# Middle stage of a fused two-layer transformer kernel: scale folded into the sign matrix, product evictions moved to ACT, second residual moved to POOL

## The chip, the cores and the metric

The kernel runs on one core of one Trainium2 chip. The metric is the device time of one execution in microseconds (us). The engines are PE (TensorE, with PEld its weight loads), DVE (VectorE), ACT (ScalarE), POOL (GpSimd) and SP, which here only issues DMAs and waits.

## What is computed

Two transformer layers on x of 4 batches, 512 tokens, 512 features, all fp32. Layer 0 has grouped causal attention with 32 heads of 128, and a feed-forward layer with a matrix of signs. Layer 1 has thresholded attention with 32 heads of 16 and a routed low-rank layer. The change is about the sign layer and the residual behind it:

```python
def _L0_ffn_ref(input, weight, scale_param):
    row_scale = jnp.clip(jnp.mean(jnp.abs(weight), axis=1), 1e-08, None)
    binary_weight = jnp.sign(weight / row_scale[:, None])
    out = jnp.einsum('bsi,oi->bso', input, binary_weight)
    out = out * row_scale[None, None, :] * scale_param[None, None, :]
    return jnp.nan_to_num(out, nan=0.0, posinf=1000000.0, neginf=-1000000.0)
...
h = _layernorm(x, axis=-1) * (1 + ca) + sa
x = x + ga * _L0_attn_ref(h, ...)
h = _layernorm(x, axis=-1) * (1 + cb) + sb
x = x + gb * _L0_ffn_ref(h, L0_ffn_weight, L0_ffn_scale_param)
...
h = _layernorm(x, axis=-1) * (1 + ca) + sa
q = (h @ Wq.T + bq)
```

## The kernel before

The batches are worked on in two halves of two. Each half goes through four stages with a barrier of all engines between them: `stage_first` (norm), `stage_groups` (attention of layer 0, by far the longest), `stage_middle` and `stage_heads_and_finish`. Only `stage_middle` is touched; it runs twice, from 846.5 us and from 1902.0 us. `x` and `y` are two SBUF buffers of eight tiles (128 tokens by 512 features each); they swap their names between the halves, so what is `y` in the first half is `x` in the rows of the second. Tiles 0 to 3 are batch 0 of the half, tiles 4 to 7 batch 1. Every engine runs its own list, written by hand, in order, and semaphores tie the lists together. There is no planner.

What `stage_middle` does in one half, tile by tile:

- The first residual, x = x + gate * attention output, is finished on DVE for tiles 4 to 7 (`summed(0, j)`: add L1319, `bn_stats` L1321); POOL does three of the gate products (L1284, semaphore `gated`).
- `normalise(i, b)` on DVE turns statistics of four tiles into mean and 1/sqrt(var) with a chain of small dependent instructions (L1341 to L1352) and raises `ready`.
- ACT's `features(i)` writes the normalised tiles (L1474), PE's `turn(i)` transposes them into PSUM (L1421), and ACT scales them on the way out (L1484; for i = 2 also L1486, the high part `hh`). Here i = 0, 1 are the inputs of the sign layer for batches 0 and 1, and i = 2, 3 those of the projections of layer 1. For i = 3 DVE writes the normalised tiles (L1382, `last_xn`).
- ACT makes the sign matrix `sgn` (L110, four slices). `signed(j)` on PE multiplies tile j with it into one of four PSUM banks `pF[j % 4]` (L1430, semaphore `full`). The order on PE is turn(0), signed(0), signed(1), turn(1), signed(2) to signed(7), turn(2), project(0) to project(6), turn(3), project(7) to project(23).
- `examine(j)` on DVE takes the product out of PSUM and multiplies it by the row scale `rs` (L1356, `z_done`, which also frees the bank), then finds NaN and infinities and replaces them (L1359 to L1365, `put`).
- POOL's `apply_gate(j)` multiplies by the second gate (L1280, `z_gated`), and DVE's `second_residual(j)` adds (L1319) and takes statistics (L1321). Behind the last tile of a batch comes `normalise(1, b)`.
- The weights of the three projections are split in a high part on ACT (`qkv.his`, L143, twelve casts) and a low part on POOL (`qkv.lo_of`, L146). POOL also makes the low part of the features (`low`, L1275, `h_lo`). `project(n)` on PE (L1450) is twelve matmuls; its first items wait slice by slice for `h_lo` and for `qkv.lo`.

The order of POOL's list and of DVE's around the sign layer, which the change touches:

```python
for j in range(TT):
    apply_gate(j)
for n in range(KT):
    qkv.lo_of(pool, n)
apply_gate(TT)
low(2, (0, 1))
apply_gate(TT + 1)
low(2, (2, 3))
apply_gate(TT + 2)
...
for j in range(TT, NT):
    first_residual(j)
normalise(0, 1)
```

Of the kernel before, what the change touches and what calls it, by code (L numbers as in the profile page):

```python
# [18 lines left out]
ALU = mybir.AluOpType  # L19
# [5 lines left out]
KT = D // P  # L25
# [93 lines left out]
class QkvWeights:  # L119
# [18 lines left out]
    def his(self, act):  # L138
        act.wait_ge(self.b_came, 48)
        for i in QKV_ORDER:  # L140
            act.wait_ge(self.came[i], 16)
            for k in range(KT):
                self.nc.scalar.copy(self.wh[:, i, k], self.raw[:, i, k]).then_inc(self.hi, 1)  # L143
# [1043 lines left out]
def stage_middle(nc, held, a, hf, signs, qkv, gates, later, kd0, half):  # L1187
# [3 lines left out]
    with Stage(nc, f"mid{half}") as st:  # L1191
# [15 lines left out]
        full, z_done, marked, replaced, put, z_gated = (st.sem(n) for n in (  # L1207
            "full", "z_done", "marked", "replaced", "put", "z_gated"))
# [30 lines left out]
        with nc.Block() as block:  # L1239

            @block.sync
            def _(sp):
                signs.load(sp)
                qkv.load(sp)
                for loaded in later:
                    loaded.load(sp)
                sp.wait_ge(own_gated, 1)
                sp.wait_ge(gated, TT - 1)
                load_gates(sp, held, a, 1, half, gate_in)
                sp.wait_ge(put, NT)  # L1250
                sp.dma_start(bo, a["b1o"].rearrange("(o d) -> o d", o=1).to_broadcast([P, D])).then_inc(bo_in, 16)
                for n, (w, b, m) in enumerate(items):
                    src = rest[n % NB]
                    if w == 2:
                        sp.wait_ge(left, n + 1)
                        for d in range(4):
                            sp.dma_start(a["vp"][b, :, :, 4 * m + d].rearrange("r g x -> g r x"),
                                         src[32 * d:32 * d + 32].rearrange("p (r x) -> p r x", r=4)).then_inc(stored[n % NB], 16)
                    else:
                        sp.wait_ge(flipped, kq[n] + 1)  # L1260
                        dst = a["kp" if w == 1 else "qp"][b, :, 4 * m:4 * m + 4].rearrange("j d l x -> (d l) j x")
                        sp.dma_start(dst, src.rearrange("p (j x) -> p j x", j=4)).then_inc(stored[n % NB], 16)
                for loaded in later:
                    loaded.landed(sp)
                for i in range(NB):
                    sp.wait_ge(stored[i], total[i])

            @block.gpsimd
            def _(pool):
# [7 lines left out]
                def apply_gate(j):  # L1277
                    pool.wait_ge(put, j + 1)
                    pool.wait_ge(gate_in, 16 * HB)
                    nc.gpsimd.tensor_tensor(y[:, j, :], y[:, j, :], gate[:, j // TT, :], ALU.mult).then_inc(z_gated, 1)  # L1280

# [28 lines left out]
            def _(dve):  # L1310
# [7 lines left out]
                def summed(i, j):  # L1318
                    nc.vector.tensor_tensor(x[:, j, :], x[:, j, :], y[:, j, :], ALU.add).then_inc(x_new, 1)  # L1319
                    dve.wait_ge(x_new, i * NT + j + 1 - TT)  # L1320
# [10 lines left out]
                def second_residual(j):  # L1331
                    dve.wait_ge(z_gated, j + 1)
                    summed(1, j)
# [20 lines left out]
                def examine(j):  # L1354
                    dve.wait_ge(full, j + 1)
                    nc.vector.tensor_tensor(y[:, j], pF[j % 4][:], rs[:], ALU.mult).then_inc(z_done, 1)  # L1356
# [12 lines left out]
                normalise(0, 1)  # L1369
                for b in range(HB):  # L1370
# [35 lines left out]
            def _(pe):  # L1406
# [17 lines left out]
                def signed(j):  # L1424
                    pe.wait_ge(signs.signed, KT)
# [41 lines left out]
            def _(act):  # L1467
                def features(i):
# [4 lines left out]
                    for j in range(b * TT, (b + 1) * TT if i < LAST else b * TT):  # L1473
                        nc.scalar.activation(y[:, j, :], x[:, j, :], ACT.Identity, bias=shifts[:, j:j + 1],  # L1474
                                             scale=scales[:, j:j + 1]).then_inc(xn_done, 1)
                    act.wait_ge(turned, i + 1)
# [31 lines left out]
                features(1)  # L1508
                qkv.his(act)
                features(2)  # L1510
                act.wait_ge(full, NT)
# [555 lines left out]
```

## Time and profile before

| what | value |
| --- | --- |
| median of 3 runs | 2157.39 us (2156.38 to 2159.48) |
| the profiled execution, its own time | 2156.57 us |
| its span, first to last instruction | 2154.6 us |
| busy share of the span: PE, DVE, ACT, POOL | 92%, 69%, 50%, 48% |
| middle stage, first half | 846.5 to about 979.2 us |
| middle stage, second half | 1902.0 to about 2035.6 us |

Busy shares are averages over stages with different limits. The two stretches of the middle stage are 12% of the span, and PE is busy for 110 and 112 us of their 133 and 134 us, so their limits are read from the timeline and not from the table. The granted clock of TensorE is written as a share of full speed: 1.00 is 2.4 GHz, 0.50 is 1.2 GHz.

### The profile page before, as it was taken

What the parts mean: (1) busy time and instruction counts of PE and PEld (TensorE: products, weight loads), DVE (VectorE), ACT (ScalarE), POOL (GpSimd) and SP (SyncE); (2) the same over time, 40 slices, a digit from 0 to 9 for tenths busy, and PEclk for the clock granted to TensorE, in tenths of its full rate; (3) what the DMA queues carried; (4) which work ended last, traced back from release to release, by engine and by line L of the source; (5) the groups of instructions that cost most, each with busy time, mean ns of one, the idle gap of its engine ahead of it and who ended that gap; (6) DMA issues with size and microseconds to landing.
All of it is one profiled execution on the core that took longest, in us unless ns stands there. A gap on an engine that the chain in (4) does not pass through costs nothing. (4 is left out here: it accounts for less than half of the span.)

```text
span 2154.6 us, 33365 instructions
## 1 busy us (share of the span) xinstructions
PE 1976.0 (92%) x11441; PEld 1605.0 (74%) x11441; DVE 1477.5 (69%) x3679; ACT 1067.6 (50%) x2422; POOL 1040.3 (48%) x801
## 2 busy tenths in 40 slices
PE   4899999999999996897948999999999999987797
PEld 3788888888888874475527888888888888745664
DVE  4666666767676666956756767676766666779386
ACT  3555555555555552433235555555556565533232
POOL 3556564655655431544046555655555565427241
PEclk7999999999999997898979999999999999988899
DMA  5010101001010234146321101010110100041561
GB/s 172 20 30 20 30 20 30 24 27 50 21 30 20 79 117 145 56 99 127 85 89 48 30 10 41 21 30 21 30 50 20 31 20 1 30 142 40 119 123 40
DMA packets 132006, 115.30 MB, mean 54 GB/s; under 512 B 43200, under 2 KB 93440, under 8 KB 131840
## 3 DMA queue, kind: packets, MB, share of 16 engines
q1 hardware_dynamic: 124784, 105.51, 17.2%
q10 hardware_dynamic: 7056, 7.68, 1.2%
q8 instruction: 93, 1.52, 0.3%
q14 instruction: 73, 0.60, 0.1%
HBM read 92.15 MB, written 16.81 MB: 51 GB/s over the span
## 5 line engine op out<-in xcount | busy, mean ns | idle before, releaser
L866 ACT ACTIVATE gqa_prob<-gqa_prob,gqa_nmax 128x256 f32<-128x256 f32 (+3 forms) x512 | 284.2, 556 | 155.1 <-DVE gqa_nmax L980 146.8
L876 ACT CAST gqa_pth<-gqa_pT 128x384 fp32r<-128x384 f32 (+1 forms) x384 | 185.4, 519 | 182.0 <-PE gqa_pT L715 179.5
L980 DVE CUSTOM_DVE_ANT_0 gqa_prob<-gqa_pS,consts 128x256 f32<-128x256 f32 (+3 forms) x512 | 222.5, 486 | 58.8 <-PE gqa_pS L677 56.7
L1149 POOL TENSOR_TENSOR x<-x,consts 128x512 f32<-128x512 f32 x80 | 107.2, 1340 | 303.4 <-ACT x L850 303.4
L1149 POOL TENSOR_TENSOR y<-y,consts 128x512 f32<-128x512 f32 x80 | 107.2, 1340 | 292.1 <-ACT y L850 292.1
L988 DVE TENSOR_TENSOR gqa_ptl<-gqa_pT,gqa_pth 128x384 fp32r<-128x384 f32 (+1 forms) x384 | 216.8, 592 | 16.8 <-ACT gqa_pth L876 16.8
L715 PE MATMUL gqa_pT<-consts,gqa_prob 128*128 128x128 f32 x1280 | 184.1, 275 | 21.7 <-DVE gqa_ptl L988 20.2
L655 PE MATMUL gqa_pj<-first_hh,wqh 128*128 128x512 f32 x496 | 196.4, 396 | 0.0
L655 PE MATMUL gqa_pj<-first_hh,wql 128*128 128x512 f32 x496 | 195.0, 393 | 0.0
L655 PE MATMUL gqa_pj<-first_hl,wqh 128*128 128x512 f32 x496 | 193.9, 391 | 0.0
L715 PEld LDWEIGHTS gqa_pT<-consts,gqa_prob 128*128 128x128 f32 x1280 | 154.3, 141 | 49.7 <-DVE gqa_prob L1004 15.8
L1004 DVE TENSOR_SCALAR gqa_prob<-gqa_prob,gqa_rden 128x128 f32<-128x128 f32 (+3 forms) x512 | 186.4, 426 | 4.6
L677 PE MATMUL gqa_pS<-gqa_kh,gqa_qh 128*128 128x256 f32 (+3 forms) x512 | 165.5, 334 | 0.0
L677 PE MATMUL gqa_pS<-gqa_kl,gqa_qh 128*128 128x256 f32 (+3 forms) x512 | 156.8, 324 | 0.0
L677 PE MATMUL gqa_pS<-gqa_kh,gqa_ql 128*128 128x256 f32 (+3 forms) x512 | 146.1, 326 | 1.5 <-POOL gqa_ql L1161 1.5
L655 PE MATMUL gqa_pj<-first_hh,wkvh 128*128 128x512 f32 x248 | 104.2, 420 | 22.5 <-PEq L83 22.5
L1000 DVE RECIPROCAL gqa_rden<-gqa_den 128x4 f32<-128x4 f32 x128 | 22.8, 178 | 136.5 <-ACT gqa_prob L866 136.5
L883 ACT CAST gqa_oh<-gqa_pS 128x512 fp32r<-128x512 f32 x64 | 37.5, 586 | 148.5 <-PE gqa_pS L726 148.5
L764 PE MATMUL gqa_pW<-woh,gqa_oh 128*128 128x512 f32 x256 | 107.5, 420 | 1.9 <-DVE gqa_ol L995 1.4
L655 PEld LDWEIGHTS gqa_pj<-first_hl,wqh 128*128 128x128 f32 x496 | 93.1, 188 | 20.7
L655 PEld LDWEIGHTS gqa_pj<-first_hh,wqh 128*128 128x128 f32 x496 | 93.1, 188 | 20.7
L655 PEld LDWEIGHTS gqa_pj<-first_hh,wql 128*128 128x128 f32 x496 | 93.1, 188 | 20.1
(341 smaller groups left out, 5454.6 us busy)
## 6 DMA issues: line engine op xcount, KB each, us to landing
raw_o<-in_wo SPq DMA_DIRECT2D x16, 1024.0 KB, 5.2
raw_q<-in_wq SPq DMA_DIRECT2D x14, 1024.0 KB, 5.6
raw_q<-in_wmod SPq DMA_DIRECT2D x10, 1024.0 KB, 5.2
raw_kv<-in_wkv SPq DMA_DIRECT2D x14, 512.0 KB, 6.9
vp<-mid_hf SPq DMA_DIRECT2D x64, 64.0 KB, 1.8
kp<-mid_hf SPq DMA_DIRECT2D x16, 256.0 KB, 2.3
qp<-mid_hf SPq DMA_DIRECT2D x16, 256.0 KB, 2.6
tail_bd<-vp SPq DMA_DIRECT2D x64, 64.0 KB, 3.3
```

Source lines behind the costliest of these rows:

```text
L655: mm = pe.matmul(bank[e][:], wp, hp[:, k, t], start=(n == 0), stop=(n == 3 * KT - 1))
L677: mm = pe.matmul(pS[s][:, c:c + wide], qp[r][:, t], kp[u % 2][:, 0:wide], start=(m == 0), stop=(m == 2))
L715: mm = pe.transpose(pT[k % 2][:, c:c + P], prob[n % 2][:, P_OFF[i] + j * P:P_OFF[i] + (j + 1) * P], held.ident)
L764: mm = pe.matmul(wbank(d)[:], op[pair % 2][:, h % 2, t], wp[:, h % R0, :], start=(m == 0), stop=(m == 5))
L866: ins = nc.scalar.activation(p, p, ACT.Exp, scale=-1.0, bias=nmax[r][:, i:i + 1], accum_out=den[r][:, i:i + 1])
L876: nc.scalar.copy(pth[:, n % 2, c:c + w], pT[k % 2][:, 0:w]).then_inc(pt_hi, 1)
L883: nc.scalar.copy(oh[p % 2][:, :, part * HALF_T:(part + 1) * HALF_T], (early, late)[part]).then_inc(o_hi, 1)
L980: nc.vector.tensor_tensor_reduce(prob[r][:, P_OFF[i]:P_OFF[i] + w], pS[s][:, c:c + w], held.mask[:, T - w:T], -1.0, LARGEST, ALU.add, ALU.min,
L988: nc.vector.tensor_tensor(ptl[:, n % 2, c:c + w], pT[k % 2][:, 0:w], pth[:, n % 2, c:c + w].bitcast(F32), ALU.subtract).then_inc(pt_lo, 1)
L1000: nc.vector.reciprocal(rden[n % 2][:], den[n % 2][:]).then_inc(recip, 1)
L1004: ins = nc.vector.tensor_scalar(p, p, rden[n % 2][:, i:i + 1], None, ALU.mult)
L1149: nc.gpsimd.tensor_tensor(rot[r % 2][:], rot[r % 2][:], held.sinT, ALU.mult).then_inc(sined, 1)
```

## The change

1. **Scale folded in.** DVE no longer multiplies each product by `rs`. Once per half, behind `normalise(0, 1)`, it multiplies the four slices of the sign matrix by `rs` in place, and `signed` on PE waits for that (`sgn_scaled`) where it waited for the signs.
2. **Products leave by ACT.** A copy on ACT (`copy(j)`) takes each product out of PSUM. The eight copies are laid between ACT's other work, and the twelve casts of `qkv.his` are cut in three portions of four.
3. **Second residual on POOL.** POOL adds right behind the gate product; DVE keeps the statistics alone, and waits for `z_added`.
4. **Second gate loaded first.** SP waits for the first gate's last use and loads the second gate (and waits for its landing, in `load_gates`) before the loads of the projection weights and the later stage's weights, not behind them.

```diff
 class QkvWeights:
-    def his(self, act):
-        act.wait_ge(self.b_came, 48)
-        for i in QKV_ORDER:
-            act.wait_ge(self.came[i], 16)
-            for k in range(KT):
-                self.nc.scalar.copy(self.wh[:, i, k], self.raw[:, i, k]).then_inc(self.hi, 1)
+    def his(self, act, nth):
+        if nth == 0:
+            act.wait_ge(self.b_came, 48)
+        i = QKV_ORDER[nth]
+        act.wait_ge(self.came[i], 16)
+        for k in range(KT):
+            self.nc.scalar.copy(self.wh[:, i, k], self.raw[:, i, k]).then_inc(self.hi, 1)
 ...
             def _(sp):
                 signs.load(sp)
+                sp.wait_ge(own_gated, 1)
+                sp.wait_ge(gated, TT - 1)
+                load_gates(sp, held, a, 1, half, gate_in)
                 qkv.load(sp)
                 for loaded in later:
                     loaded.load(sp)
-                sp.wait_ge(own_gated, 1)
-                sp.wait_ge(gated, TT - 1)
-                load_gates(sp, held, a, 1, half, gate_in)
 ...
                     nc.gpsimd.tensor_tensor(y[:, j, :], y[:, j, :], gate[:, j // TT, :], ALU.mult).then_inc(z_gated, 1)
+                    pool.wait_ge(z_gated, j + 1)
+                    nc.gpsimd.tensor_tensor(x[:, j, :], x[:, j, :], y[:, j, :], ALU.add).then_inc(z_added, 1)
 ...
                 def summed(i, j):
-                    nc.vector.tensor_tensor(x[:, j, :], x[:, j, :], y[:, j, :], ALU.add).then_inc(x_new, 1)
-                    dve.wait_ge(x_new, i * NT + j + 1 - TT)
+                    if i == 0:
+                        nc.vector.tensor_tensor(x[:, j, :], x[:, j, :], y[:, j, :], ALU.add).then_inc(x_new, 1)
+                        dve.wait_ge(x_new, j + 1 - TT)
                     nc.vector.bn_stats(stats[:, i, j, :], x[:, j, :]).then_inc(stat_done, 1)
 ...
                 def second_residual(j):
-                    dve.wait_ge(z_gated, j + 1)
+                    dve.wait_ge(z_added, j + 1)
 ...
                 def examine(j):
-                    dve.wait_ge(full, j + 1)
-                    nc.vector.tensor_tensor(y[:, j], pF[j % 4][:], rs[:], ALU.mult).then_inc(z_done, 1)
                     dve.wait_ge(z_done, j + 1)
 ...
                 normalise(0, 1)
+                for k in range(KT):
+                    dve.wait_ge(signs.signed, k + 1)
+                    nc.vector.tensor_tensor(sgn[:, k], sgn[:, k], rs[:], ALU.mult).then_inc(sgn_scaled, 1)
 ...
                 def signed(j):
-                    pe.wait_ge(signs.signed, KT)
+                    pe.wait_ge(sgn_scaled, KT)
 ...
             def _(act):
+                def copy(j):
+                    act.wait_ge(full, j + 1)
+                    nc.scalar.copy(y[:, j], pF[j % 4][:]).then_inc(z_done, 1)
+
-                def features(i):
+                def features(i, between=()):
 ...
+                    for j in between:
+                        copy(j)
                     act.wait_ge(turned, i + 1)
 ...
-                features(1)
-                qkv.his(act)
-                features(2)
-                act.wait_ge(full, NT)
+                features(1, (0, 1))
+                copy(2)
+                qkv.his(act, 0)
+                copy(3)
+                qkv.his(act, 1)
+                copy(4)
+                qkv.his(act, 2)
+                copy(5)
+                features(2, (6, 7))
```

DVE's list in the first half, from the end of `normalise(0, 1)` on. The names are output<-inputs; `mid_pF` is a PSUM bank with a product. Before:

```order
L1352 SCALAR_TENSOR_TENSOR mid_shift<-mid_mv,mid_rstd 128x4
L1356 TENSOR_TENSOR y<-mid_pF,rs 128x512
L1359 TENSOR_TENSOR mid_nan<-y 128x512
L1360 TENSOR_SCALAR mid_clip<-y 128x512
L1361 TENSOR_SCALAR mid_wild<-y 128x512
L1363 COPY_PREDICATED y<-mid_wild,mid_clip 128x512
L1365 COPY_PREDICATED y<-mid_nan,consts 128x512
```

Now:

```order
L1356 SCALAR_TENSOR_TENSOR mid_shift<-mid_mv,mid_rstd 128x4
L1374 TENSOR_TENSOR sgn<-sgn,rs 128x512 x4
L1361 TENSOR_TENSOR mid_nan<-y 128x512
L1362 TENSOR_SCALAR mid_clip<-y 128x512
L1363 TENSOR_SCALAR mid_wild<-y 128x512
L1365 COPY_PREDICATED y<-mid_wild,mid_clip 128x512
L1367 COPY_PREDICATED y<-mid_nan,consts 128x512
```

Four instructions with both inputs in SBUF now stand between the normalisation and the first tile, and the one with the PSUM input is gone from each of the eight tiles.

POOL's list in the first half, from the gate product of tile 4 on. Before:

```order
L1280 TENSOR_TENSOR y<-y,gate 128x512
L1275 TENSOR_TENSOR second_hl<-mid_hf,second_hh 128x512 x2
L1280 TENSOR_TENSOR y<-y,gate 128x512
L1275 TENSOR_TENSOR second_hl<-mid_hf,second_hh 128x512 x2
L1280 TENSOR_TENSOR y<-y,gate 128x512
L146 TENSOR_TENSOR qkv_wl<-qkv_raw,qkv_wh 128x512 x2
L1280 TENSOR_TENSOR y<-y,gate 128x512
L146 TENSOR_TENSOR qkv_wl<-qkv_raw,qkv_wh 128x512 x6
```

Now:

```order
L1281 TENSOR_TENSOR y<-y,gate 128x512
L1283 TENSOR_TENSOR x<-x,y 128x512
L1276 TENSOR_TENSOR second_hl<-mid_hf,second_hh 128x512 x2
L1281 TENSOR_TENSOR y<-y,gate 128x512
L1283 TENSOR_TENSOR x<-x,y 128x512
L1276 TENSOR_TENSOR second_hl<-mid_hf,second_hh 128x512 x2
L1281 TENSOR_TENSOR y<-y,gate 128x512
L1283 TENSOR_TENSOR x<-x,y 128x512
L147 TENSOR_TENSOR qkv_wl<-qkv_raw,qkv_wh 128x512 x2
L1281 TENSOR_TENSOR y<-y,gate 128x512
L1283 TENSOR_TENSOR x<-x,y 128x512
L147 TENSOR_TENSOR qkv_wl<-qkv_raw,qkv_wh 128x512 x6
```

Each gate product is followed by an add of the same size, ahead of the low parts that PE waits for.

## Rows read from the trace of the kernel before

**Rows 1.** A window: length, busy PE, PEld, DVE, ACT, POOL, clock, DMA share, GB/s

```profile
895.00:925.00 30.00, 22.49 (x87) 16.71 (x88) 29.14 (x46) 11.88 (x15) 22.63 (x15) 0.86 0.19 45
```

**Rows 2.** Timeline of PE: start, duration us, engine, line, what [idle before, releaser]

```profile
855.69 8.78 PE L1430 MATMUL mid_pF<-sgn,mid_hf 128*128 128x512 f32 x16 [4.95 <-ACT sgn L110]
...
866.05 20.77 PE L1430 MATMUL mid_pF<-sgn,mid_hf 128*128 128x512 f32 x48
890.91 3.64 PE L1421 MATMUL mid_pT<-consts,y 128*128 128x128 f32 x16 [4.09 <-ACT y L1474]
900.11 0.80 PE L1450 MATMUL mid_pT<-second_hh,qkv_wh 128*128 128x512 f32 x1 [5.55 <-ACT second_hh L1486]
...
917.59 0.50 PE L1450 MATMUL mid_pT<-second_hh,qkv_wh 128*128 128x512 f32 x1 [0.72 <-POOL qkv_wl L146]
...
924.73 1.94 PE L1421 MATMUL mid_pF<-consts,y 128*128 128x128 f32 x16 [0.57 <-DVE y L1382]
...
1911.32 10.02 PE L1430 MATMUL mid_pF<-sgn,mid_hf 128*128 128x512 f32 x16 [4.94 <-ACT sgn L110]
```

**Rows 3.** Timeline of DVE in the first half

```profile
857.81 0.16 DVE L1352 SCALAR_TENSOR_TENSOR mid_shift<-mid_mv,mid_rstd 128x4 f32<-128x4 f32 x1
861.07 0.69 DVE L1356 TENSOR_TENSOR y<-mid_pF,rs 128x512 f32<-128x512 f32 x1 [3.10 <-PE mid_pF L1430]
...
864.60 0.68 DVE L1356 TENSOR_TENSOR y<-mid_pF,rs 128x512 f32<-128x512 f32 x1
...
879.70 0.73 DVE L1365 COPY_PREDICATED y<-mid_nan,consts 128x512 f32<-128x512 int32 x1
...
885.00 0.36 DVE L1341 BATCH_NORM_AGGREGATE mid_mv<-mid_stats 128x2 f32<-128x6 f32 x4
...
924.04 1.91 DVE L1382 TENSOR_SCALAR y<-x,mid_mv,mid_rstd 128x512 f32<-128x512 f32 x4
```

**Rows 4.** One line's instructions: count, ns min/median/max, first and last start

```profile
L1356 DVE TENSOR_TENSOR y<-mid_pF,rs x8: 673/680/690, 861.1 to 906.8; 128x512 f32<-128x512 f32 x8
L1319 DVE TENSOR_TENSOR x<-x,y x12: 666/856/1650, 848.4 to 915.4; 128x512 f32<-128x512 f32 x12
L1360 DVE TENSOR_SCALAR mid_clip<-y x8: 412/420/1516, 862.4 to 909.0; 128x512 f32<-128x512 f32 x8
L1321 DVE BATCH_NORM_STATS2 mid_stats<-x x12: 693/694/695, 850.0 to 916.4; 128x6 f32<-128x512 f32 x12
L1280 POOL TENSOR_TENSOR y<-y,gate x8: 1267/1625/1718, 871.1 to 912.5; 128x512 f32<-128x512 f32 x8
L1812 ACT COPY tail_sc<-tail_pS x32: 567/598/625, 988.7 to 2082.1; 128x512 f32<-128x512 f32 x32
```

**Rows 5.** Timeline of POOL in the first half

```profile
893.56 1.27 POOL L1280 TENSOR_TENSOR y<-y,gate 128x512 f32<-128x512 f32 x1 [5.63 <-DVE y L1365]
896.12 3.49 POOL L1275 TENSOR_TENSOR second_hl<-mid_hf,second_hh 128x512 fp32r<-128x512 f32 x2 [1.29 <-ACT second_hh L1486]
...
905.64 1.65 POOL L1280 TENSOR_TENSOR y<-y,gate 128x512 f32<-128x512 f32 x1 [1.47 <-DVE y L1365]
...
912.54 1.64 POOL L1280 TENSOR_TENSOR y<-y,gate 128x512 f32<-128x512 f32 x1 [2.31 <-DVE y L1365]
914.13 8.40 POOL L146 TENSOR_TENSOR qkv_wl<-qkv_raw,qkv_wh 128x512 fp32r<-128x512 f32 x6
```

**Rows 6.** Timeline of ACT, of SP and of POOL: normalised tiles out, gate load, first gating

```profile
889.96 2.93 ACT L1474 ACTIVATE y<-x,mid_shift,mid_rstd 128x512 f32<-128x512 f32 x4 [14.71 <-DVE mid_shift L1352]
894.60 0.78 ACT L1484 ACTIVATE mid_hf<-mid_pT,modT 128x512 f32<-128x512 f32 x1 [1.71 <-PE mid_pT L1421]
861.38 3.40 SPq L217 DMA_DIRECT2D gate<-gates  x2
871.06 2.69 POOL L1280 TENSOR_TENSOR y<-y,gate 128x512 f32<-128x512 f32 x2 [19.92 <-DMA gate<-gates]
```

**Rows 7.** DMA issues: bytes of each, median us from issue to landing

```profile
qkv_raw<-in_w1q SPq DMA_DIRECT2D x2, 1024.0 KB, 10.6
```

More of the change, by code:

```diff
@@ L1206, in stage_middle @@
         LAST = 2 * HB - 1
-        full, z_done, marked, replaced, put, z_gated = (st.sem(n) for n in (
-            "full", "z_done", "marked", "replaced", "put", "z_gated"))
+        full, z_done, marked, replaced, put, z_gated, z_added, sgn_scaled = (st.sem(n) for n in (
+            "full", "z_done", "marked", "replaced", "put", "z_gated", "z_added", "sgn_scaled"))
         gate_in = st.sem("gate_in")
```

## The prediction

> **What bounds the kernel now.** I read the windows first, to see how much of the kernel the change can reach: two stretches of 133 us, 12% of the span. Then the timeline of PE inside the first stretch, since the sign products and the projections are PE's, and from each of its pauses the timeline of the engine that ended it. From 924.73 us on, PE works through its last 17 projections without a pause that the trace shows, so the end of the stretch moves one for one with the time at which the fourth transposition (`turn(3)`) starts. Ahead of it PE has four waits that count [rows 2]: 4.95 us for the signs from ACT, 4.09 us for the normalised tiles, 5.55 us for the scaled features, and short ones for POOL's low parts (0.72 us at 917.59) and for DVE's last normalised tile (0.57 us at 924.73). The chain behind them is: sign products, DVE's examination of tile 3, gate, residual, `normalise`, ACT's tiles (889.96), PE's transposition, ACT's features, first projection (900.11). Then POOL's list runs until 922.53 (914.13 + 8.40), and DVE's normalisation ends behind it, at 924.04 [rows 3, 5]. In the stretch from 895 to 925 DVE is busy for 29.14 of 30 us and POOL for 22.63, PE for 22.49 [rows 1].
>
> The two busy engines hinder each other, and this decides the case. `L1360` takes 0.42 us at the median and 1.52 at most; an add with both inputs in SBUF (`L1319`) takes 0.67 at least and 1.65 at most; `L1356`, which reads PSUM and one SBUF tile, never strays from 0.67 to 0.69 [rows 4], beside a busy POOL too. A DVE instruction that meets a POOL instruction waits for it: 1.52 - 0.42 = 1.10 us for one collision. POOL's gate product takes 1.27 us alone and 1.62 at the median.
>
> **The change part by part.** I walk the first half.
>
> *Start of the sign products.* They waited for the signs, until 855.69. Now four multiplications by `rs` come between, and they stand on DVE behind `normalise(0, 1)`, which ends at 857.97 (857.81 + 0.16). POOL is idle there, so 4 x 0.67 = 2.7 us [rows 3, 4]: PE starts at about 860.75, **5.1 us later**.
>
> *Tile 3.* Before, PE was not what held DVE at tile 3; now it is. From PE's start to its third tile 10.36 us pass (855.69 to 866.05), and a tile takes 20.77 / 6 = 3.46 us [rows 2]. Product 3 is complete at 860.75 + 10.36 + 6.92 = 878.0. ACT's copy is not in this trace; ACT's nearest copy, PSUM to SBUF at the same size, takes 0.60 us, and it ends near 878.7. The four casts ahead of it on ACT fit in the tile's time. A tile on DVE took 3.53 us (861.07 to 864.60), without `L1356` (0.73 with its handoff) 2.80. So the tile is put at 881.5 if POOL is out of the way, against 880.43 (879.70 + 0.73) before. It isn't: gate and add of tiles 1 and 2 run just then, and I take two collisions, 2.2 us. **+3.3**; ends +1.1 and, with a third collision, +4.4.
>
> Here the trace and a rule can be weighed. The rows say that SBUF pairs collide and the PSUM reader doesn't. The Trainium skill, "SBUF — State Buffer", section "Who interferes with whom", says that a DVE instruction with two SBUF inputs or in a two-port mode and a GpSimd instruction that reads SBUF exclude each other for a whole instruction, and that one with at most one SBUF input doesn't contend. By it the change takes away the eight DVE instructions that never collided and puts eight more colliding ones on POOL. A collision would be a whole POOL instruction, 1.27 us, and this step +3.6 in place of +3.3.
>
> *Gate and residual of tile 3.* Before, 4.57 us from 880.43 to the first aggregate at 885.00: POOL's product beside DVE's add and statistics of three tiles. Now POOL's product, POOL's add and one `bn_stats` in a chain: 1.27 + 1.27 + 0.69 = 3.2, or with 1.62 each and handoffs 4.1. The add on POOL is bounded by the gate product, the same shape. **-0.9**, ends -1.3 and -0.4. `normalise` keeps POOL's four low parts beside it and its length.
>
> *Copies 6 and 7* stand on ACT between the normalised tiles and the features: 2 x 0.6 = 1.2 us, where ACT waited 1.71 us for PE [rows 6]. **0**. If that cover shrinks, since PE may transpose at a higher clock, they cost at most what they save. Copies 0 to 5 lie in ACT's idle time of 14.71 us.
>
> *POOL up to its last low part.* From 893.56 to 922.53 it idles 1.29 + 1.47 + 2.31 = 5.07 us [rows 5]. Four adds bring 4 x 1.27 = 5.1 to 4 x 1.62 = 6.5 us. The first two stand ahead of low parts that the first projection waits for, the others ahead of those that the fifth waits for. **+1.0**, ends 0 and +1.4. DVE has its PSUM reads and adds off, so it stays ahead of POOL; its last normalisation still follows POOL's end by 1.5 us (922.53 to 924.04).
>
> *Clock.* Eight sign matmuls (16 records) at full speed are 8 x 20.77 / 24 = 6.9 us; they took 8.78 us in the first half and 10.02 in the second, both after 4.9 us without PE work [rows 2]. The pause is now 10 us. The slow part may be as short or as long as either: 0 to +1.2, I take **+0.6**.
>
> *Gate load.* It lands 871.06 before, behind all other loads; now it is there when tile 0 is put. POOL gains 2.7 us on tiles 0 and 1 and then waits for DVE anyway: 0. On SP it is moved ahead of eleven other loads. SP waits for the end of the first gating (851.14: POOL's idle of 19.92 us before 871.06 begins there), issues for 3.40 us and waits for a landing (6.28 us: 861.38 + 3.40 to 871.06) [rows 6], until 860.8. Five issues stand ahead of the last projection weight; at 1.7 us each, half of that 3.40 and surely too much, it is issued by 869.3 and lands 10.6 us later [rows 7], by 880. Its casts come behind copy 4, near 882. **0**, with 2 us of cover at the worst; without it every us late would be one on `lo_of`.
>
> Sum for a half: 3.3 - 0.9 + 0 + 1.0 + 0.6 = **+4.0 us**. The second half has the same lists: +8.0. The profiled execution (2156.57 us, 2154.6 us of span and 2.0 around it) would come to 2164.6; it stands 0.8 below the median of 2157.39, so I forecast **2165 us** for the median, to the nearest us.
>
> **The rivals.** A change within 0.2%, 4.3 us, is what this kernel's measurement can't tell from none.
>
> *No change.* The late start costs only the 1.1 us of step two, since collisions fall beside waits, and the shorter tail of step three pays it back: -0.2 to +2.1 a half, 2157 to 2161.5. For it: DVE had waited 3.10 us for PE ahead of tile 0 and loses nothing by waiting longer for a shorter list. Against: eight more POOL instructions in stretches where both are nearly full.
>
> *Faster: DVE's relief decides.* DVE is the fullest engine from 895 to 925. If `normalise(1, 0)` ends no later than before (steps two and three together 0 or below), tiles 4 to 7 are put 0.73 us earlier each, POOL's list moves up, and PE's waits for POOL and DVE (0.72 at 917.59, 0.57 at 924.73 and one like them before) vanish: -2.2 a half, **2153 us**. It needs the late start to be absorbed wholly, and in my walk tile 3 alone is late by 1.1 us without any collision.
>
> *Much slower: POOL becomes the bound.* If the adds cannot use the idle times, as gate and add wait for a DVE that they hold up themselves, all of 6.5 us comes on the path from tile 4 on, with no gain in step three: +6.5 to +7, 2171 us. The skill's rule above speaks for it, since it is exclusive both ways.
>
> *The change doesn't do what it says.* The casts could run dry for want of weights, because the loads now start some 10 us later. It would need the last to land after 882, 2 us behind my late estimate; each us beyond is one a half.
>
> **How the numbers follow.** My forecast has 0.55 (2162 to 2169), no change 0.20, faster 0.10, POOL as the bound 0.12, late weights 0.03. The range drops half of the faster case at the bottom and half of the slowest at the top: all steps at their low ends and the clock at zero give -0.2 a half, a part of the relief another -0.8, so 2155.5; the high ends 4.4 - 0.4 + 1.4 + 1.2 = 6.6 give 2170.6, so 2171. Faster by over 0.2%: 0.10; within: 0.20; slower: 0.70.
>
> **What would show it.** In the changed profile: PE's first sign matmul near 860.75, released by DVE's `sgn` multiplication; tile 3's last `COPY_PREDICATED` 2 to 4 us later than 879.70; ACT's third set of normalised tiles near 892; PE waiting on POOL's `second_hl` in the first projection; `turn(3)` near 928.7, and PE without a pause behind it. I am wrong if ACT's tiles start before 890, if `turn(3)` is not late, or if DVE's statistics never wait for POOL's add; and wrong about the cause if the time is right and PE's first sign matmul is not late.

## The result, and the profile after

| | before | after |
| --- | --- | --- |
| median of 9 runs | 2157.89 us | 2168.65 us |
| ratio of after to before | | 1.0057, 95% interval 1.0044 to 1.0071 |
| the profiled execution, its own time | 2156.57 us | 2167.60 us |
| its span | 2154.6 us | 2165.4 us |
| `turn(0)` to `turn(3)` on PE, first and second half | 77.36, 78.32 us | 84.19, 83.34 us |

The kernel is slower, by 10.8 us in the median. (The ratio is pulled up by one run of 2183.72 us among the nine of after.) The last row of the table is the measure used below: from the start of PE's first transposition of the middle stage to the start of its fourth. Those two stretches grew by 6.83 and 5.02 us, 11.85 in all. The rest of the span varies by some 6 us between the profiled executions of this document (1996.8 to 2002.9 us), with no order by edit, and was 1.05 us shorter in this one.

The timeline of PE in the kernel after (start, duration, engine, line, what, [idle before, releaser]), against [rows 2]. The line numbers have moved: sign products L1435, transpositions L1426, projections L1455.

```profile
848.27 3.24 PE L1426 MATMUL mid_pT<-consts,y 128*128 128x128 f32 x16 [2.54 <-ACT y L1483]
861.33 9.93 PE L1435 MATMUL mid_pF<-sgn,mid_hf 128*128 128x512 f32 x16 [9.82 <-DVE sgn L1374]
...
897.38 3.43 PE L1426 MATMUL mid_pT<-consts,y 128*128 128x128 f32 x16 [3.77 <-ACT y L1483]
906.36 0.80 PE L1455 MATMUL mid_pT<-second_hh,qkv_wh 128*128 128x512 f32 x1 [5.55 <-ACT second_hh L1497]
910.63 0.79 PE L1455 MATMUL mid_pT<-second_hh,qkv_wh 128*128 128x512 f32 x1 [1.33 <-POOL second_hl L1276]
...
932.46 1.94 PE L1426 MATMUL mid_pF<-consts,y 128*128 128x128 f32 x16 [0.36 <-DVE y L1387]
...
1921.27 9.03 PE L1435 MATMUL mid_pF<-sgn,mid_hf 128*128 128x512 f32 x16 [9.53 <-DVE sgn L1374]
```

The first half's middle stage began 0.90 us later in this execution (848.27 for 847.37), so 0.90 is taken off every difference. The sign products start 861.33 - 855.69 - 0.90 = 4.74 us later, released by DVE's multiplication. The third transposition is 5.57 later, the first projection 5.35, the fourth transposition 6.83. Behind the loss of the start, 0.8 us was lost up to the third transposition (5.57 - 4.74) and 1.5 from the first projection on (6.83 - 5.35). In the second half the same four differences are 4.61, 3.96, 3.92 and 5.02.

The timeline of DVE, against [rows 3]: the four multiplications, tile 0, tile 3, and tile 5.

```profile
858.78 2.49 DVE L1374 TENSOR_TENSOR sgn<-sgn,rs 128x512 f32<-128x512 f32 x4
868.48 0.69 DVE L1361 TENSOR_TENSOR mid_nan<-y 128x512 int32<-128x512 f32 x1 [7.21 <-ACT y L1475]
...
882.29 1.42 DVE L1361 TENSOR_TENSOR mid_nan<-y 128x512 int32<-128x512 f32 x1
883.62 1.49 DVE L1362 TENSOR_SCALAR mid_clip<-y 128x512 f32<-128x512 f32 x1
885.04 0.41 DVE L1363 TENSOR_SCALAR mid_wild<-y 128x512 int32<-128x512 f32 x1
...
886.28 0.74 DVE L1367 COPY_PREDICATED y<-mid_nan,consts 128x512 f32<-128x512 int32 x1
...
889.74 0.69 DVE L1325 BATCH_NORM_STATS2 mid_stats<-x 128x6 f32<-128x512 f32 x1 [1.56 <-POOL x L1283]
...
899.12 0.68 DVE L1361 TENSOR_TENSOR mid_nan<-y 128x512 int32<-128x512 f32 x1
899.71 1.50 DVE L1362 TENSOR_SCALAR mid_clip<-y 128x512 f32<-128x512 f32 x1
901.13 1.49 DVE L1363 TENSOR_SCALAR mid_wild<-y 128x512 int32<-128x512 f32 x1
902.65 1.68 DVE L1365 COPY_PREDICATED y<-mid_wild,mid_clip 128x512 f32<-128x512 int32 x1
904.37 1.65 DVE L1367 COPY_PREDICATED y<-mid_nan,consts 128x512 f32<-128x512 int32 x1
905.92 0.67 DVE L1361 TENSOR_TENSOR mid_nan<-y 128x512 int32<-128x512 f32 x1
```

And POOL's, against [rows 5], with ACT's copy of tile 3 and its third set of normalised tiles, against [rows 6]:

```profile
881.89 1.26 POOL L1281 TENSOR_TENSOR y<-y,gate 128x512 f32<-128x512 f32 x1 [2.28 <-DVE y L1367]
883.23 1.60 POOL L1283 TENSOR_TENSOR x<-x,y 128x512 f32<-128x512 f32 x1
...
899.32 1.61 POOL L1281 TENSOR_TENSOR y<-y,gate 128x512 f32<-128x512 f32 x1 [4.72 <-DVE y L1367]
901.01 1.33 POOL L1283 TENSOR_TENSOR x<-x,y 128x512 f32<-128x512 f32 x1
902.37 3.06 POOL L1276 TENSOR_TENSOR second_hl<-mid_hf,second_hh 128x512 fp32r<-128x512 f32 x2
...
879.91 0.58 ACT L1475 COPY y<-mid_pF 128x512 f32<-128x512 f32 x1 [0.78 <-PE mid_pF L1435]
...
896.42 2.93 ACT L1483 ACTIVATE y<-x,mid_shift,mid_rstd 128x512 f32<-128x512 f32 x4 [9.05 <-DVE mid_shift L1356]
```

Read the two together. In these lines each POOL instruction meets one DVE instruction, which lasts longer than its usual time: tile 3 has two long ones (1.42 for 0.69, 1.49 for 0.42) beside gate and add of tile 2, tile 5 four of them beside gate and add of tile 4 and two low parts. Tile 5 takes 905.92 - 899.12 = 6.80 us, where in the kernel before tile 5 took 5.03 with one instruction more. Tile 3's product was in SBUF at 880.49 (879.91 + 0.58), and DVE began with it at 882.29: DVE was still at tile 2, whose examination met a gate and an add too.

### The profile page after: what moved, and what is told of

It is laid out like the page before. It is cut to its first block and busy times, and to the rows that moved or that the text cites. A ratio compares the mean times of both kernels' runs of the same rounds, so it can differ in the third digit from the quotient of the medians.

```text
span 2165.4 us, 33369 instructions
## 1 busy us (share of the span) xinstructions
PE 1978.0 (91%) x11441; PEld 1607.2 (74%) x11441; DVE 1479.5 (68%) x3655; ACT 1076.9 (50%) x2438; POOL 1057.5 (49%) x817
## 5 line engine op out<-in xcount | busy, mean ns | idle before, releaser
L989 DVE TENSOR_TENSOR gqa_ptl<-gqa_pT,gqa_pth 128x384 fp32r<-128x384 f32 (+1 forms) x384 | 217.0, 593 | 16.9 <-ACT gqa_pth L877 16.9
```

Source lines behind the costliest of these rows:

```text
L989: nc.vector.tensor_tensor(ptl[:, n % 2, c:c + w], pT[k % 2][:, 0:w], pth[:, n % 2, c:c + w].bitcast(F32), ALU.subtract).then_inc(pt_lo, 1)
```

## The experiments

All times are medians. The kernel before stood beside each set: 2157.58 us (21 runs) for e1 to e4, 2156.89 (24) for e5 to e8, 2155.80 (12) for e9 to e12. The change is median minus that median; the stretch is `turn(0)` to `turn(3)` in either half, and the last column the sum of both against the profiled kernel before (155.68).

| kernel | median us (runs) | ratio, 95% interval | change | stretch | sum |
| --- | --- | --- | --- | --- | --- |
| after | 2168.65 (9) | 1.0057 (1.0044 to 1.0071) | +10.8 | 84.19, 83.34 | +11.9 |
| e1 | 2166.46 (5) | 1.0036 (1.0022 to 1.0049) | +8.9 | 81.47, 81.33 | +7.1 |
| e2 | 2159.76 (11) | 1.0009 (1.0000 to 1.0018) | +2.2 | 79.50, 79.75 | +3.6 |
| e3 | 2160.00 (11) | 1.0012 (1.0003 to 1.0020) | +2.4 | 78.26, 79.04 | +1.6 |
| e4 | 2169.15 (5) | 1.0055 (1.0043 to 1.0068) | +11.6 | 84.55, 83.33 | +12.2 |
| e5 | 2154.12 (10) | 0.9986 (0.9974 to 0.9998) | -2.8 | 76.80, 75.20 | -3.7 |
| e6 | 2167.81 (6) | 1.0046 (1.0032 to 1.0060) | +10.9 | 82.32, 83.01 | +9.7 |
| e7 | 2149.81 (5) | 0.9964 (0.9949 to 0.9979) | -7.1 | 73.61, 75.01 | -7.1 |
| e8 | 2151.47 (12) | 0.9971 (0.9962 to 0.9981) | -5.4 | 74.86, 75.07 | -5.8 |
| e9 | 2163.29 (5) | 1.0034 (1.0021 to 1.0047) | +7.5 | 80.66, 80.69 | +5.7 |
| e10 | 2173.93 (5) | 1.0081 (1.0068 to 1.0094) | +18.1 | 86.01, 86.61 | +16.9 |
| e11 | 2169.03 (5) | 1.0057 (1.0044 to 1.0069) | +13.2 | 83.68, 83.68 | +11.7 |
| e12 | 2149.55 (8) | 0.9967 (0.9956 to 0.9977) | -6.3 | 74.10, 74.36 | -7.2 |

### e1: the scaling ahead of the normalisation

```diff
-                normalise(0, 1)
                 for k in range(KT):
                     dve.wait_ge(signs.signed, k + 1)
                     nc.vector.tensor_tensor(sgn[:, k], sgn[:, k], rs[:], ALU.mult).then_inc(sgn_scaled, 1)
+                normalise(0, 1)
```

> The changed kernel, with the four multiplications of the sign matrix ahead of normalise(0, 1) on DVE, not behind it. If the late start of the sign products is a full part of the loss, PE's first sign matmul comes 2.9 us earlier (near 858.5 on the clock of the changed kernel's profile, the length of the normalisation), every step behind it moves with it, and the time falls by 2.5 to 3 us a half: about 2163 where the changed kernel has 2168.7. If the collisions of DVE and POOL alone decide, and the start is absorbed in DVE's 7 us of waiting ahead of tile 0, nothing moves: 2168 to 2169. The batch 1 tiles of ACT are 2.5 us later in either case and are not needed before PE has done two tiles.

PE's first sign product starts 10.13 us behind `turn(0)` in place of 13.06 (2.9 us earlier, as expected), and the stretches are 2.7 and 2.0 us shorter than after's. The time, 2166.46 us, missed the 2163 that was expected: the medians differ by 2.2 us, less than the intervals are wide, and the stretches by 4.7.

### e2: the second residual back on DVE

```diff
-                    pool.wait_ge(z_gated, j + 1)
-                    nc.gpsimd.tensor_tensor(x[:, j, :], x[:, j, :], y[:, j, :], ALU.add).then_inc(z_added, 1)
 ...
-                    if i == 0:
-                        nc.vector.tensor_tensor(x[:, j, :], x[:, j, :], y[:, j, :], ALU.add).then_inc(x_new, 1)
+                    nc.vector.tensor_tensor(x[:, j, :], x[:, j, :], y[:, j, :], ALU.add).then_inc(x_new, 1)
```

> The changed kernel with the second residual's add back on DVE; scale folded in, copies on ACT and gate first stay. If POOL's adds are the larger part of the loss (each collides with DVE's examination, and 4 of them lengthen POOL's list ahead of its last low part), tile 3 is put about 2.5 us earlier, POOL's last low part ends about 5 us earlier, and the time is 2158 to 2160, no slower than the kernel before within 0.1%. If the late start alone decides, it stays near 2166 to 2168.

Most of the loss is gone: +2.2 us is left of +10.8. Having the sixteen adds on POOL and not on DVE costs 8.6 us.

### e3: no scaling

The multiplication by the row scale is left out altogether.

```diff
-                for k in range(KT):
-                    dve.wait_ge(signs.signed, k + 1)
-                    nc.vector.tensor_tensor(sgn[:, k], sgn[:, k], rs[:], ALU.mult).then_inc(sgn_scaled, 1)
 ...
-                    pe.wait_ge(sgn_scaled, KT)
+                    pe.wait_ge(signs.signed, KT)
```

> The changed kernel without the multiplication by the row scale (that part of the computation is left out), so PE starts on the bare signs. If the start's delay is passed on in full, 4.7 us less a half plus what the shorter pause gives back in clock: 2158 to 2160. If DVE's and POOL's collisions absorb a part of an earlier start, 2161 to 2165. If the start is not on the path, 2168.

So the scaling and the late start that it brings cost 8.4 us, with the adds still on POOL. That and the price of the adds (e2) come to 17.0 us, more than the whole loss. If the two are independent, something in the change must gain, and e7 looks for it.

### e4: the gate load behind the weights again

```diff
-                sp.wait_ge(own_gated, 1)
-                sp.wait_ge(gated, TT - 1)
-                load_gates(sp, held, a, 1, half, gate_in)
                 qkv.load(sp)
                 for loaded in later:
                     loaded.load(sp)
+                sp.wait_ge(own_gated, 1)
+                sp.wait_ge(gated, TT - 1)
+                load_gates(sp, held, a, 1, half, gate_in)
```

> The changed kernel with the second gate's load behind the weights again. By my account the order of the loads is worth nothing either way: in this kernel tile 0 is put at 871.4, when the gate of the kernel before had landed. 2168 to 2169. If the late weight loads had cost, or the early gate had gained, over 1 us a half would show: below 2166.5 or above 2170.5.

2169.15 against 2168.65 us: in this kernel the order of the loads makes no difference that the times can show. Tile 0 is put at 871.38 here (870.64 + 0.74), no earlier than the gate had landed in the kernel before (871.06), so e4 says nothing about a kernel whose sign products start early.

### e5: both e1 and e2

> The changed kernel with both cures: the multiplications of the sign matrix ahead of normalise(0, 1), and the add of the second residual on DVE. From the stage's start to the fourth transposition the first of them alone took 2.7 and 2.0 us off the two halves and the second 4.7 and 3.6. If the two costs lie in series on one chain they add up: 2155 to 2156, 1.5 to 3 us below the kernel before. If an earlier start is only worth something beside POOL's adds, it stays at the 2159.8 of the residual on DVE alone.

-2.8 us against before; the 2154.12 us are 1 to 2 us below what was expected. With the adds on DVE, putting the scaling first is worth 5.0 us (e2 to e5), more than beside the adds on POOL (e1), and the adds on POOL cost 11.7 (e1 to e5). So the two costs are not strictly additive.

### e6: the kernel before, with the adds on POOL alone

The edit of e2, the other way round, in the kernel before; products still leave PSUM through DVE.

> The kernel before with one part of the change alone: POOL adds the second residual. If the adds cost by colliding with DVE's examination, they cost here too, where PE starts early: 3 to 4.5 us a half, 2164 to 2167. If they cost only in company with the late start (because DVE then has no waiting time of its own), 2158 to 2161.

+10.9 us, as much as the whole change, though the parts differ, and slightly over the 2164 to 2167 us that were expected. The timeline of DVE, tile 5 and then the last normalisation of the first half:

```profile
896.57 0.69 DVE L1359 TENSOR_TENSOR y<-mid_pF,rs 128x512 f32<-128x512 f32 x1
897.28 1.29 DVE L1362 TENSOR_TENSOR mid_nan<-y 128x512 int32<-128x512 f32 x1
898.50 1.48 DVE L1363 TENSOR_SCALAR mid_clip<-y 128x512 f32<-128x512 f32 x1
899.90 1.50 DVE L1364 TENSOR_SCALAR mid_wild<-y 128x512 int32<-128x512 f32 x1
901.44 1.69 DVE L1366 COPY_PREDICATED y<-mid_wild,mid_clip 128x512 f32<-128x512 int32 x1
903.16 0.74 DVE L1368 COPY_PREDICATED y<-mid_nan,consts 128x512 f32<-128x512 int32 x1
...
925.07 1.21 DVE L1352 TENSOR_TENSOR mid_step<-mid_rstd 128x4 f32<-128x4 f32 x1
...
928.81 0.16 DVE L1352 TENSOR_TENSOR mid_step<-mid_rstd 128x4 f32<-128x4 f32 x1
```

Tile 5 takes 7.2 us for 5.03 before: four instructions are lengthened where two were. `L1359`, which reads PSUM, is not. Even 128x4 instructions of the normalisation take 1.21 us in place of 0.16 while POOL works.

### e7: after without the scaling, and with the adds on DVE

The row scale is left out here too. What remains of the change is the copies on ACT and the gate load.

> The changed kernel with neither the multiplication by the row scale (left out) nor POOL's add, so what is left is the product leaving by ACT and DVE freed of eight PSUM reads. In series the two costs give 11.8 - 10.2 - 8.3 = -6.7 us against the kernel before: 2151. If DVE's relief is worth less than that, because PE's pace of 3.46 us a tile and POOL's list hold the chain by then, 2153 to 2157.

-7.1 us. So copies on ACT and the early gate load, together, are the part of the change that gains. One cause is at hand: DVE is rid of its eight PSUM reads in each half, 0.73 us each with the handoff. The other is the gate. In the kernel before, POOL began its first gate product at 871.06, when the gate landed [rows 6], and its two products ran beside DVE's tile 2:

```profile
871.10 1.52 DVE L1360 TENSOR_SCALAR mid_clip<-y 128x512 f32<-128x512 f32 x1
```

In e7 the gate is there early, POOL is released by DVE's tile 0, and tile 2 meets nothing:

```profile
865.89 1.27 POOL L1281 TENSOR_TENSOR y<-y,gate 128x512 f32<-128x512 f32 x1 [13.55 <-DVE y L1364]
...
872.21 0.42 DVE L1359 TENSOR_SCALAR mid_clip<-y 128x512 f32<-128x512 f32 x1
```

With `mid_wild` (1.49 before, 0.42 in e7) that is 2.2 us of tile 2, where the first half's stretch is 3.75 us shorter; in the second half it is 1.5 us of 3.31. So a good part of the gain may be the gate load's and not the copies'. No run has an early start with only one of the two, and how the 7.1 us divide is not shown.

### e8: e5, and PE waits for the scaled signs slice by slice

```diff
-                    pe.wait_ge(sgn_scaled, KT)
 ...
                     for k in range(KT):
+                        if j == 0:
+                            pe.wait_ge(sgn_scaled, k + 1)
                         mm = pe.matmul(pF[j % 4][:], hf[j // TT][:, k, j % TT * P:(j % TT + 1) * P], sgn[:, k, :],
```

> A candidate: scaling ahead of normalise(0, 1), PE's first tile waiting for the sign matrix slice by slice, and the add on DVE. PE should start about 0.8 us later than in the kernel before, not 4.7, and a cold matmul (1.7 us) hides the 0.6 us that each further slice takes. In series: 2152 to 2154, faster than both kernels. If the earlier start is absorbed by POOL's list: 2155 to 2158.

PE's timeline shows the start back where it was, 8.41 us behind `turn(0)` (8.32 in the kernel before, 13.06 after):

```profile
847.12 3.38 PE L1423 MATMUL mid_pT<-consts,y 128*128 128x128 f32 x16 [2.55 <-ACT y L1481]
855.53 8.50 PE L1433 MATMUL mid_pF<-sgn,mid_hf 128*128 128x512 f32 x16 [5.03 <-DVE sgn L1370]
...
921.98 1.94 PE L1423 MATMUL mid_pF<-consts,y 128*128 128x128 f32 x16 [0.58 <-DVE y L1384]
```

The start is almost wholly restored, and the kernel is faster than both, with the full computation (2151.47 us; 2152 to 2154 was expected). 1.7 us are left to e7, which has no scaling at all.

### e9: the kernel before, POOL adds only for tiles 4 to 7

```diff
+                    if j >= TT:
+                        pool.wait_ge(z_gated, j + 1)
+                        nc.gpsimd.tensor_tensor(x[:, j, :], x[:, j, :], y[:, j, :], ALU.add).then_inc(z_added, 1)
```

> The kernel before, with POOL adding the second residual of tiles 4 to 7 only (tiles 0 to 3 stay on DVE). All eight tiles on POOL cost +10.9 us in the kernel before. Theory A (the adds lengthen POOL's list, and the low parts and the last normalisation stand at its end): nearly all of it comes back here, +7 to +11 us. Theory B (the chain behind tile 3 decides, since ACT's tiles and the first projection wait for it): this kernel keeps that chain, so only +0 to +4 us.

+7.5 of e6's +10.9: two thirds of the price come with the adds of tiles 4 to 7, where POOL's list also holds the low parts.

### e10: the kernel before, one more add that nobody waits for

```diff
                     nc.gpsimd.tensor_tensor(y[:, j, :], y[:, j, :], gate[:, j // TT, :], ALU.mult).then_inc(z_gated, 1)
+                    nc.gpsimd.tensor_tensor(qkv.wl[:, 0, j % KT], gate[:, 0, :], gate[:, 1, :], ALU.add).then_inc(junked, 1)
```

> The kernel before, with one more POOL add of 128x512 behind each gate product, of the two gate tiles into a buffer that is still free; nobody waits for it but POOL's own later list, and DVE keeps its adds. POOL is as full as in the kernel with the adds moved, and DVE is fuller. Theory A (occupancy: a longer list on POOL and collisions with DVE): +8 to +14 us, at least what moving the adds cost (+10.9). Theory B (latency: DVE waits through gate and add in a chain): +0 to +4 us, as nothing waits for the new adds.

+18.1 us, more than even the occupancy theory allowed (+8 to +14). So the chain from gate through add to statistics is not needed for the price; one more instruction on POOL brings it, though no other engine waits for it. Moving the adds (e6) costs 7.2 us less than this; that DVE is rid of its own adds there is the likely reason (sixteen of at least 0.67 us, 10.7 us of DVE's work), but no run separates it.

### e11: the same place, a memset

```diff
+                    if j:
+                        pool.wait_ge(junked, j)
+                    nc.gpsimd.memset(qkv.wl[:, 0, 0:3].bitcast(F32), 0.0).then_inc(junked, 1)
```

> The same place, but a memset of 128x1536 in place of the extra add: about as long (1.3 to 1.4 us for POOL) and it reads nothing. If the collisions of POOL's reads with DVE are the price, DVE's instructions keep their short durations beside it and it costs much less than the extra add, +0 to +4 us where that costs +8 or more. If POOL's longer list alone is the price, both cost the same within 2 us.

+13.2 us: neither of the two expectations came out. It is not nearly free, as collisions of reads alone would have it, and it costs 4.9 us less than the add. The timelines of DVE and of POOL show what the memset meets:

```profile
913.34 0.69 DVE L1363 TENSOR_TENSOR mid_nan<-y 128x512 int32<-128x512 f32 x1
913.94 0.79 DVE L1364 TENSOR_SCALAR mid_clip<-y 128x512 f32<-128x512 f32 x1
...
1937.23 0.95 DVE L1363 TENSOR_TENSOR mid_nan<-x 128x512 int32<-128x512 f32 x1
1938.11 1.13 DVE L1364 TENSOR_SCALAR mid_clip<-x 128x512 f32<-128x512 f32 x1
1939.16 2.81 DVE L1365 TENSOR_SCALAR mid_wild<-x 128x512 int32<-128x512 f32 x1
...
1945.42 0.69 DVE L1363 TENSOR_TENSOR mid_nan<-x 128x512 int32<-128x512 f32 x1
1946.03 0.76 DVE L1364 TENSOR_SCALAR mid_clip<-x 128x512 f32<-128x512 f32 x1
```

```profile
913.08 1.37 POOL L1283 MEMSET qkv_wl<- 128x1536 f32 x1
...
1936.35 1.28 POOL L1280 TENSOR_TENSOR x<-x,gate 128x512 f32<-128x512 f32 x1 [19.89 <-DMA gate<-gates]
1937.58 1.38 POOL L1283 MEMSET qkv_wl<- 128x1536 f32 x1
1938.91 1.45 POOL L1280 TENSOR_TENSOR x<-x,gate 128x512 f32<-128x512 f32 x1
1940.31 1.37 POOL L1283 MEMSET qkv_wl<- 128x1536 f32 x1
...
1945.14 1.38 POOL L1283 MEMSET qkv_wl<- 128x1536 f32 x1
```

`mid_nan`, with two SBUF inputs, runs through a memset at its own 0.69 us (913.34 inside 913.08 to 914.45, and again at 1945.42); the 0.95 us at 1937.23 began beside a gate product, which reads (1936.35 to 1937.63). `mid_clip`, a `TENSOR_SCALAR` of 0.42 us, lasts until just behind the end of the memset. `mid_wild` at 1939.16 lasts through a gate product and the memset behind it, 2.81 us. The prediction's reading that SBUF pairs collide was too narrow: `mid_clip` and `mid_wild` have one input each. This is what the Trainium skill, "SBUF — State Buffer", section "Who interferes with whom", states: two SBUF inputs contend with a GpSimd instruction that reads, not with one that only writes, and a `tensor_scalar` in a two-port mode contends with either. The trace agrees on both.

### e12: e8, with the last four low parts behind the last normalisation

```diff
-                for n in range(KT + 2, 3 * KT):
+                for n in range(KT + 2, 2 * KT):
+                    qkv.lo_of(pool, n)
+                pool.wait_ge(ready, 3)
+                for n in range(2 * KT, 3 * KT):
                     qkv.lo_of(pool, n)
```

> The fastest kernel so far (scale first, slice by slice; add on DVE; 2151.5 us), with POOL's last four low parts held back until the last normalisation has its scales. Theory A: the small dependent instructions of the last normalisation wait for POOL one by one, so it shrinks from about 6 to 7 us to 3 to 4, and the last transposition starts up to 1 us earlier in each half: -1 to -3 us. Theory B: the transposition is held by PE's own projections and by POOL's earlier low parts, so nothing is gained: 0 within 0.5 us. If the late low parts come too late for the ninth projection, +2 us or more.

The timeline of DVE, last normalisation and its tiles, in e12:

```profile
913.66 0.36 DVE L1345 BATCH_NORM_AGGREGATE mid_mv<-mid_stats 128x2 f32<-128x6 f32 x4
...
916.51 0.16 DVE L1356 SCALAR_TENSOR_TENSOR mid_shift<-mid_mv,mid_rstd 128x4 f32<-128x4 f32 x1
916.59 4.83 DVE L1387 TENSOR_SCALAR y<-x,mid_mv,mid_rstd 128x512 f32<-128x512 f32 x4
```

and in e8:

```profile
914.29 0.36 DVE L1342 BATCH_NORM_AGGREGATE mid_mv<-mid_stats 128x2 f32<-128x6 f32 x4
...
921.29 1.91 DVE L1384 TENSOR_SCALAR y<-x,mid_mv,mid_rstd 128x512 f32<-128x512 f32 x4
```

The normalisation shrinks from 7.0 to 2.9 us, but the low parts now fall beside the four tiles, which take 4.83 for 1.91. The stretches are 0.8 and 0.7 us shorter than e8's, 1.5 us together, within the -1 to -3 us that were expected. The ratios (0.9967, 0.9971) don't separate the two, so that e12 beats e8 is not shown by the times; that both beat the kernel before is.

## Why the prediction was right, and where it was wrong

The direction, the place and the time within its range were right: 2165 forecast, 2168.65 measured. The stretches grew by 11.9 us where the sum had 8.0, so the size came out near the upper end. PE did wait for the `sgn` multiplication, for `second_hl` in the first projection, and DVE's statistics for POOL's add; but tile 3, ACT's third set of tiles and `turn(3)` came 2.4 to 3.5 us later than the prediction wrote (5.7 us of delay for 3.3, 896.42 - 0.90 = 895.5 for 892, 932.46 - 0.90 = 931.6 for 928.7). By the predicted steps, first half, each relative to the stage's start:

- *Start of the sign products*: +5.1 forecast, +4.74 measured, released by DVE's `sgn` multiplication as said.
- *Clock*: +0.6 forecast; the first sign products took 9.93 for 8.78 us (+1.15) in the first half and 9.03 for 10.02 (-1.0) in the second. Over all runs, pauses of 4.9 to 10.3 us ahead of them gave 8.5 to 10.2 us. The three kernels with a pause near 10 us (after, e2, e4) had 9.9 to 10.2 us in the first half, where pauses near 5 us had 8.5 to 10.0, but 9.0 to 9.3 in the second, where those had 9.2 to 10.2. So over both halves it is about 0, and no run bears out the +0.6.
- *Tile 3 put*: +3.3 forecast, 886.28 - 879.70 - 0.90 = +5.7 measured, 1.15 of it the clock. Tile 3's two collisions were foreseen, at 2.2 us, and cost 1.8 (0.73 + 1.07). Another 1.8 us went where DVE started tile 3 after its product was ready, since tile 2 had been lengthened as well (1.31 for 0.69, 1.49 for 0.42). Tile 1's delay was still absorbed: DVE waited 0.59 us for ACT ahead of tile 2. The step's claim that PE now holds DVE at tile 3 was wrong.
- *Gate and residual*: -0.9 forecast, -1.2 measured (886.28 to 890.35, where 879.70 to 885.00 stood).
- *Normalise keeps its length*: it took 6.07 us for 4.96, +1.1, since three of its small instructions met a POOL instruction and not two.
- *Copies 6 and 7*: 0, as forecast; ACT's tiles to the first projection is 9.94 us, 10.15 before.
- *POOL up to its last low part*: +1.0 forecast (0 to +1.4). From the first projection to `turn(3)` it was +1.5 in the first half and +1.1 in the second.
- *Gate load*: 0 forecast, 0 measured (e4).

**The term that was mis-sized** is the price of the adds on POOL. In the sum they stood for 2.2 (collisions) - 0.9 + 1.0 = +2.3 us a half. e2 against after, e6 against before and e5 against e1 give 8.6, 10.9 and 11.7 us, that is 4.3 to 5.9 a half. The remaining part, late start with DVE's relief and without the adds, was forecast at +1.1 and +0.6 for the clock, 3.4 in all; e2 measured +2.2 us in the median and +3.6 in the stretches. So the walk through the late start came out to the size of the noise, and the adds cost about twice what was put down. Collisions were counted for tile 3 alone. But tiles 1, 2 and 3 had two each and took 4.5 to 4.6 us on DVE against PE's 3.43, so that DVE fell behind from tile 2 on, and tile 5 had four for two before. That the total still came within 3.7 us is in small part luck: the clock's +0.6 a half, which the runs do not show, stood in for a part of what the adds lacked.

What the walk kept as one net number is three large ones: copies on ACT with the early gate -7.1 (e7), the scaling and the start behind it +8.4 to +9.3 (after to e3, e7 to e2), the adds +8.6 to +9.5 in the changed kernel (after to e2, e3 to e7), and 10.9 and 11.7 elsewhere (e6, e5 to e1). Along one path they add up to the whole by construction (-7.1 + 9.3 + 8.6 = +10.8). What the runs do show is that in the changed kernel each of the two costs is within 1 us the same, whether the other is there or not.

Of the rivals, *faster* named DVE's relief; a gain of that place exists (e7), how much of it is the relief is open, and both losses outweigh it. *POOL becomes the bound* was the nearest miss: it gave the adds 6.5 us a half from tile 4 on, and e9 measured 3.75. It also named exclusion in both directions as its reason; after's rows have both engines' instructions lengthened side by side, DVE's `mid_clip` 1.49 for 0.42 and POOL's add 1.60 for 1.26 to 1.33. *No change* is excluded by the time. *Late weights* is excluded by the profile and by e4: ACT's last casts of the weights ended at 886.0 in the first half, each set right behind its copy.

What is open: how e6's +10.9 divides between longer DVE instructions and a longer list of POOL, since no run took one without the other (e11 only lessens the first); and how e7's -7.1 divides between the copies and the gate load.

## What to carry to other kernels

Before work is moved from DVE to POOL, count the instructions with SBUF inputs on both engines in the stretch, not the busy shares: in this stretch, where both are nearly full, one more POOL instruction of 1.3 us cost about 1.1 us (e10: 16 of them, 18.1 us), even where no other engine waited for it. Taking PSUM evictions off DVE for ACT gained here, together with an earlier gate. But a step put at the head of a chain in exchange should be hidden (first on its engine, and handed on slice by slice): behind the normalisation it cost 9.3 us (e7 to e2), and hidden 1.7 (e7 to e8). A term that is a net of gains and losses should be split and each part priced.

## What the runs showed of the hardware

- Beside a POOL `TENSOR_TENSOR`, one DVE instruction after the other is lengthened by up to about a POOL instruction: 0.69 to 1.29-1.42, 0.42 to 1.49, and a conditional copy from 0.74 to 1.7 us (after, e6). One in e11 lasted through two, 2.81 us for 0.42. DVE's PSUM reads (0.67 to 0.69) and its `bn_stats` (0.67 to 0.70) were never lengthened in any run.
- Small DVE instructions are hit as well: 128x4 ones go from 0.16 to 1.21 us, though not all of them. A chain of small dependent instructions took 7.0 us beside POOL and 2.9 without it (e8 and e12).
- A memset on POOL spares DVE's instructions with two inputs, not its `TENSOR_SCALAR` (e11).
- ACT's copy of 128x512 from PSUM takes 0.56 to 0.59 us in every run that has it, beside busy POOL and DVE too.
